# Starting the second expert pass inside the last attention of a macaron block

## What is computed

```python
def ffn(tgt):                      # 8 experts, the best 2 of each row
    logits = tgt @ Wr.T + br
    top_v, top_i = top_k(logits, 2)
    h = relu(tgt @ W1[e].T + b1[e])            # 128 -> 512
    o = h @ W2[e].T + b2[e]                    # 512 -> 128
    return layer_norm(tgt + sum of weight * o) * gamma + beta

def attn(x):                       # per batch
    a1 = softmax(q1 @ k1.T * scale); a2 = softmax(q2 @ k2.T * scale)
    out = (a1 - lam * a2) @ v
    return out / rms(out) * 0.2

x = x + 0.5 * ffn(layernorm(x))
x = x + attn(layernorm(x))
x = x + 0.5 * ffn(layernorm(x))
```

## Time and profile before

| | |
|---|---|
| runs | 649.92 us, median of 3 (648.65 to 650.58) |
| profiled execution | 649.61 us, span 647.9 us |
| TensorE busy | 583.2 us, 90% of the span |
| VectorE, ScalarE, GpSimd busy | 452.0, 446.3, 387.4 us |
| mean granted TensorE clock | 0.959 |
| the last attention | up to about 450 us |
| the second pass | from about 450 us to 614 us |

### The profile page before, as it was taken

One profiled execution on the slowest core, in us unless ns is written; L12 is line 12 of the kernel. 1 busy time (PEld: TensorE's weight loads), 2 busy tenths in 40 slices (PEclk: granted clock), 3 DMA queues, 4 the chain that ended last, 5 costly groups with the idle time before them and its releaser, 6 DMA issues.

```text
span 647.9 us, 16591 instructions
## 1 busy us (share of the span) xinstructions
PE 583.2 (90%) x4362; PEld 536.0 (83%) x4362; DVE 452.0 (70%) x1421; ACT 446.3 (69%) x1224; POOL 387.4 (60%) x481
## 2 busy tenths in 40 slices
PE   5987999999999789898898899887999999899855
PEld 5877999999999678787797788787999999898821
DVE  4784788446684989699779968966647565477635
ACT  4755665766667577677887787675776777787724
POOL 3006565547677785678505486585775777756623
PEclk9588999999999999899999999998999999999958
DMA  8902233223324210000000001021441423630051
GB/s 254 326 12 57 77 77 72 79 69 88 84 68 82 53 30 14 18 24 22 5 2 0 6 30 34 18 69 31 95 103 58 102 79 80 216 95 26 24 194 66
DMA packets 41882, 45.97 MB, mean 71 GB/s; under 512 B 8726, under 2 KB 32706, under 8 KB 41536
## 3 DMA queue, kind: packets, MB, share of 16 engines
q1 hardware_dynamic: 32496, 27.13, 14.6%
q0 software_dynamic: 9088, 17.75, 10.3%
q10 hardware_dynamic: 208, 0.02, 0.0%
HBM read 25.95 MB, written 19.83 MB: 71 GB/s over the span
## 4 chain that ended last, share of the span: by engine, by line
PE 55%; DVE 19%; ACT 8%; issue 7%; POOL 6%; DMA 3%; ACTq 1%; SPq 0%; DVEq 0%; POOLq 0%
PE banks L1074 19%; PE banks L1084 19%; DVE nb L1837 6%; DVE scratch L1844 3%; PE banks L1067 2%; PE banks L1171 2%; PE banks L962 2%; PE banks L964 2%; PE banks L963 2%; POOL rows L499 1%; DVE st_r L1334 1%; POOL zb L512 1%; ACT tgt L649 1%; DVE st_x L1334 1%; DVE mv L1340 1%
## 5 line engine op out<-in xcount | busy, mean ns | idle before, releaser
L1074 PE MATMUL banks<-scratch 128*128 128x128 f32 x1248 | 169.1, 279 | 1.8 <-ACT scratch L706 1.6
L1084 PE MATMUL banks<-blocks,scratch 128*128 x1248 | 166.3, 276 | 2.6 <-ACT scratch L713 1.3
L1587 DVE TENSOR_SCALAR scratch<-banks,blocks 128x128 f32<-128x128 f32 x312 | 95.2, 346 | 91.6 <-PE banks L1074 80.8
L1074 PEld LDWEIGHTS banks<-scratch 128*128 128x128 f32 x1248 | 154.6, 195 | 4.4 <-issue 4.1
L1084 PEld LDWEIGHTS banks<-blocks,scratch 128*128 128x128 f32 x1248 | 151.8, 192 | 4.9 <-issue 4.6
L491 POOL DMA_INDIRECT scratch<-xrows,rowbuf x78 | 75.2, 965 | 82.0 <-DVE rowbuf L1482 41.4
L697 ACT ACTIVATE scratch<-banks 128x128 f32<-128x128 f32 x156 | 43.5, 279 | 88.8 <-PE banks L1067 87.9
L788 ACT ACTIVATE scratch<-banks,nb 128x1024 f32<-128x1024 f32 x64 | 71.3, 1115 | 47.7 <-DVE nb L1837 47.3
L524 POOL DMA_INDIRECT results<-scratch,places x78 | 78.4, 1005 | 34.7 <-issue 21.3
L713 ACT ACTIVATE scratch<-banks,blocks 128x128 f32<-128x128 f32 x312 | 96.8, 366 | 1.2 <-PE banks L1074 1.1
L706 ACT ACTIVATE scratch<-blocks 128x512 f32 x156 | 97.5, 625 | 0.1
(11 more groups left out here) (265 smaller groups left out, 896.5 us busy)
## 6 DMA issues: line engine op xcount, KB each, us to landing
scratch<-rows SPq DMA_DIRECT2D x78, 64.5 KB, 1.9
yrows<-scratch SPq DMA_DIRECT2D x78, 64.0 KB, 1.7
scratch<-in_L_ffn_W_dram SPq DMA_DIRECT2D x1, 2048.0 KB, 20.7
xrows<-tgt SPq DMA_DIRECT2D x4, 512.0 KB, 4.3
x<-in_L_attn_x_dram SPq DMA_DIRECT2D x3, 512.0 KB, 7.9
scratch<-xrows,rowbuf POOLq DMA_INDIRECT x78, 2.6
results<-scratch,places POOLq DMA_INDIRECT x78, 2.4
rows<-padrows SPq DMA_DIRECT2D x18, 64.5 KB
```

What stands on the lines that cost most here:

```text
L1074: ins = pe.matmul(hT_at(T, c), staged(T, c), xT_of(T), start=True, stop=True)
L1084: ins = pe.matmul(y_at(T), hT_of(T, c), blocks[:, W2_AT + c * D:][:, bass.ds(at, D)], start=(c == 0), stop=(c == FC - 1))
L1587: ins = dve.tensor_scalar(hT_of(T, c), hT_at(T, c), blocks[:, B1_AT + c:][:, bass.ds(at, 1)], 0.0, ALU.add, ALU.max)
```

## The change

The first two turns of the second pass and its first product are moved from the head of the pass into the end of the last attention. On TensorE the turn of slot 78 comes ahead of `values` of tile 30, the turn of slot 79 and `first` of slot 78 come ahead of `values` of tile 31, and the pass's loop begins with s = 0 after a wait for `ss_ready` of all 32 tiles. ScalarE's steps -2 and -1 go along, and `copy_rows` of batch 2 comes after them instead of ahead of `take_o` of tile 30. SyncE's one wait on 32 turned tiles becomes three, on 30, 31 and 32 tiles, ahead of the first three loads; for this the three buffers `p1` are used in another order. VectorE's first `add_values` of the last batch moves into the pass's step 0, and the routing of batch 3 moves back by one slot (STATS_AT 1, TURN_AT 9).

```diff
-        STATS_AT, TURN_AT = 0, 8
+        STATS_AT, TURN_AT = 1, 9
...
             group_ready(0)
-            sp.wait_ge(dT_ps, TB * BATCHES)
             for s in range(SLOTS):
+                if s < 3:
+                    sp.wait_ge(dT_ps, TB * BATCHES - 2 + s)
...
# ScalarE, probabilities (and in the same way in turn and difference)
-                    pp, ll = ((p1[t % 3], l1), (p2[t % 2], l2))[m]
+                    pp, ll = ((p1[(t + 2) % 3], l1), (p2[t % 2], l2))[m]
...
# ScalarE, end of the attention
-                if not after:
                     dT_copy(b, TB - 1)
-                    copy_rows(b - 1)
+                    act.wait_ge(table_ready, 3)
+                    step(1, -2)
                     take_o(b, TB - 2)
                     gap(a)
+                    step(1, -1)
+                    copy_rows(b - 1)
                     take_o(b, TB - 1)
...
-            for s in range(-2, SLOTS):
+            for s in range(SLOTS):
                 step(1, s)
...
# TensorE, end of the attention
                     turn(b, TB - 1)
+                    pe.wait_ge(table_ready, 3)
+                    turn_x(SLOTS)
+                    w_at[0] = expert_offset(PE, 0)
                     values(b, TB - 2)
                     prefix(a)
+                    turn_x(SLOTS + 1)
+                    w_at[1] = expert_offset(PE, 1)
+                    first(SLOTS)
                     values(b, TB - 1)
...
-            pe.wait_ge(table_ready, 3)
-            for s in range(-2, SLOTS):
+            pe.wait_ge(ss_ready, TB * BATCHES)
+            for s in range(SLOTS):
...
# VectorE
             def last_route(n):
+                add_values(b, 0)
+                yield
                 add_values(b, 1)
...
-                if not after:
-                    add_values(b, 0)
...
-                if s >= STATS_AT:
+                if s >= STATS_AT - 1:
                     next(routing, None)
```

More of the change, by code:

```diff
@@ L1151, in turn @@
                 for k in range(TB):
-                    ins = pe.transpose(bank(4 + k // 4, (k % 4) * P, (k % 4 + 1) * P), p1[t % 3][:, k * P:(k + 1) * P], ident[:, :])
+                    ins = pe.transpose(bank(4 + k // 4, (k % 4) * P, (k % 4 + 1) * P), p1[(t + 2) % 3][:, k * P:(k + 1) * P], ident[:, :])
                 ins.then_inc(dT_ps, 1)
@@ L1842, in difference @@
                     dve.wait_ge(cc_ready, TB * b + i + 1)
-                    pp = p1[(TB * b + i) % 3]
+                    pp = p1[(TB * b + i + 2) % 3]
                     dve.scalar_tensor_tensor(pp, p2[i % 2], cc[:, c], pp, ALU.mult, ALU.add).then_inc(diff_ready, 1)
```

## The result

The changed kernel takes 658.16 us (median of four runs, 655.88 to 660.13) against 649.28 for the kernel before: 1.0138 times as long, 95% interval 1.0113 to 1.0163, or some 8.9 us more. Its profiled execution took 657.71 us, with a span of 656.0. The forecast was 657.8.

A forecast was written before the change was run, and what follows sets the result against it. TensorE, busy 583 of 647.9 us, was taken to bound the kernel, with the pass started by a load behind GpSimd's last scatter. A shift of +8.2 (6.3 loop, 1.9 slot) on 649.61 gave 657.8 us, range 654.3 to 661.0.

The forecast's parts named there:

- The load isn't released by the split wait but by the last scatter: SyncE at the seam: the split wait is met by 442.4, the scatter's wait ends at 446.83; gain 0.
- 7.3 us of idle time: TensorE ahead of the turn of slot 78: idles from 442.4 to 449.7, waiting for the first load.
- Values of tile 30 at half clock, 3.8 us: TensorE behind the first turn: values of tile 30 take 3.8 us at the low clock, against 2.02 at 2.4 GHz.
- `ss_ready` +8.65, TensorE +5.1 at step 1: End of the seam: last take_o ends at 459.0, not 450.32; step 1's turn comes at 461.1, not 455.98.
- `nm` decides when `make_rows` starts, +8.2, after a wait of 1.4 us: Routing of batch 3: GpSimd's nm ready at 473.65, 1.4 us after ScalarE is ready; make_rows starts at 473.75, +8.2 us.
- The gate 504.7 and the fetch 565.2, both +8.2: GpSimd's first scatter of batch 3 moves from 496.49 to 504.7; batch 0's result comes at 565.2; the loop is +8.2.
- After it TensorE and ScalarE go on as before.: Behind the fetch of batch 0: nothing later gives any of the +8.2 us back; the time from 504 shifts as a block.
- The total: Whole kernel: profiled execution 649.61 us plus 8.2 gives 657.8 us; chance of this case, 656 to 660, 0.62.
- only TensorE's own lateness: Rival: the slot later is swallowed or the clock is high; +5.1 to +6.3, 654.7 to 655.9 us; chance 0.20.
- Its price for a high clock at the seam, 1.9 us: Same rival, values of tile 30 at 2.4 GHz: work from 450.2 to 454 and the end shrink by 1.9 us, +6.3.
- Faster, if the load is there first: Rival at the seam: early rows let turns and product fill the wait, the clock stays high; 646.6 us; chance 0.05.
- Fixed cost of a load: SyncE's first load: lands after 1.80 us by the trace; about 2.0 by the skill, making the sum an estimated +8.4.

The follow-up runs named there:

- e8: The kernel before with only SyncE's wait split into three and the p1 buffers in the other order; 649.13 us, ratio 1.0003.
- e9: The changed kernel without the last three scatters of batch 1, with padding rows written ahead of the attention; 654.62 us, ratio 1.0073.
- e7: The changed kernel with the routing of batch 3 back at its old slots (STATS_AT 0, TURN_AT 8); 658.83 us, ratio 1.0141.
- e4: The changed kernel with 34 transposes of the identity on TensorE ahead of the turn of slot 78; 659.47 us, ratio 1.0154.
- e1: The kernel before with only the routing of batch 3 one slot later and the last batch's add_values inside the pass; 653.52 us, ratio 1.0068.
- e3: The kernel before with GpSimd's last three batch 1 scatters ahead of value_scale and the last batch's first add_values inside the pass; 650.08 us, ratio 1.0006.
- e2: The changed kernel with GpSimd's last three scatters of batch 1 ahead of value_scale of tiles 24 to 27; 655.75 us, ratio 1.0106.
- e5: The changed kernel with values of tile 30 and the prefix ahead of the turn of slot 78, ScalarE likewise; 656.34 us, ratio 1.0113.
- e11: The changed kernel with 62 transposes of the identity on TensorE ahead of the turn of slot 78; 656.98 us, ratio 1.0106.
- e10: The kernel before without the last three scatters of batch 1, with padding rows written ahead of the attention; 654.98 us, ratio 1.0081.

## Why the prediction was right, point by point

- *The load isn't released by the split wait but by the last scatter.* Shown: issued at +6.46 us with the split (e8) and +6.50 without, and with the last three scatters away the first turn is at 0.9 us (e9).
- *7.3 us of idle time.* Measured 7.41. The idle time that it replaces was misread: ahead of the second turn has 0.83 us and not 1.2. Nothing in the sum hangs on it.
- *Values of tile 30 at half clock, 3.8 us.* Measured 3.75, and 2.02 with TensorE kept active. The clock came back 13.6 us after the last turn began, I had 12.6; the product took 1.13 us all the same.
- *`ss_ready` +8.65, TensorE +5.1 at step 1.* Measured +8.5, and the turn of step 1 at 19.8 against 14.6 us, +5.2.
- *`nm` decides when `make_rows` starts, +8.2, after a wait of 1.4 us.* Measured +8.0 with a wait of 0.68. Shown by e7. The wait, for which I had given over 1 us as a sign, was shorter because ScalarE itself was 0.6 us later than in my sum and `nm` 0.2 us sooner.
- *The gate 504.7 and the fetch 565.2, both +8.2.* Measured +8.0 and +8.3. GpSimd waited 3.76 us at the gate, as before, for a later slot table. ScalarE's wait at the fetch, which was to be above 5 us, was 4.53, as ScalarE came there 0.9 us later than in my sum.
- *"After it TensorE and ScalarE go on as before."* Here the sum was off: +9.6 at the end, not +8.3, so the time behind the gate was not shifted as one block. In the changed kernel the stop at the fetch was longer and the clock fell behind it. From ScalarE's start on batch 0's result to the last turn of the pass it is 51.6 us in the four profiles where the clock stayed up there (before, e4, e7, e8; TensorE stood 0.57 to 2.16 us), and 52.9 to 53.2 us in the nine where it fell (2.28 to 3.67 us). So the fall costs 1.3 to 1.6 us. Behind the last turn of the pass it is 38.9 to 39.3 us to the end of the span in all but e4: the changed kernel gets back 0.4 us there (39.0 against 39.3), which leaves +1.3. In e4 the clock fell once more in this last part (a product at 643.94 took 2.04 us behind a stop of 2.84; the same one in e7 took 1.13 us behind 1.94), and it took 40.6 us. The fall at the fetch also explains most of why e1's end is 1.0 us later than its fetch, and why e3's gain came to nothing.
- *The total.* That 657.8 lies 0.4 us from the measured 658.16 is in part luck. Counted from the last turn, the end is 9.6 us later where I had 8.2. But the profiled execution of the changed kernel reached that turn 1.46 us sooner (439.91 against 441.37), by the spread between executions told of above, so that the two profiled executions differ by only 8.1 us; the medians differ by 8.9.
- *Among the rivals,* "only TensorE's own lateness" is out for the changed kernel: its gate and its fetch came late with the sums (+8.5, +8.0, +8.3), and in e2, e5 and e11 all three came sooner together, by 2.0 to 2.4 us. Its price for a high clock at the seam, 1.9 us, was about right: e11 has 2.2. "Faster, if the load is there first" had its condition right and its gain too high: I had 3.0 us ahead of the kernel before (646.6 against 649.61), and e9, counted from the last turn, is 2.2 us ahead at the gate and level at the end of the span.
- *Fixed cost of a load.* The loads land after 1.9 us (median of the changed kernel's 78), near the 1.80 of my row. The Trainium skill, DMA: Bandwidth & Descriptors, Anatomy of one DMA, has about 2.0 us, but for DMAs that GpSimd issues, and SyncE issues these; no run here tests the figure. With the same page's rule to wait on a DMA's semaphore late, under Rules for kernel authors, the changed kernel agrees (the wait ahead of the work, +9 us), and e9 bounds it: where the load has landed, an early wait costs nothing.

## What to carry to other kernels

Before work is pulled ahead of a boundary, find what releases its input, not only which wait stands in front of it: of two waits in a row only the later one is worth splitting. A turn whose load is 7 us away must not stand ahead of work that doesn't need it, and the price is not the idle time but the lateness of the next thing that the other engines go by. A shift that is handed on from gate to gate can grow where the clock falls behind a stop, so a sum of shifts has to take in the stops behind it too.

## What the runs showed of the hardware

- TensorE's granted clock fell to the 1.2 GHz level behind a stop of 2.26 us ahead of the prefix in the kernel before, of 2.28 us at the fetch in e10, of 2.36 us in e3 and of 2.88 us in e7. It stayed at 2.4 GHz through 2.16 us at the fetch in the kernel before and 2.08 in e7, but also through 2.27 us ahead of the prefix in e10 (its lines stand below). So the length of one stop doesn't tell by itself whether the clock falls; what else decides was not tested. A fall at the fetch cost 1.3 to 1.6 us of work on top of the stop.
- Three indirect scatters issued directly behind `ratio` took longer: the first held GpSimd for 2.09 us in e2 and e3 (1.16 in the kernel before, behind the 2.8 us of `value_scale`), and in e3 the last landed after 3.19 us instead of 2.34. The cause was not tested. A reordering on GpSimd that should have gained 2.9 us gained 0.9 to 1.6.
- Transposes of the identity took 0.11 us each at full clock (62 in 6.93 us). With 62 in the wait, which left 0.62 us of idle time behind them, the values ran at full clock; with 34, which left 3.53 us, they ran at half clock as without any.

The stop of e10 ahead of the prefix, and the values of tile 31 behind it at full clock:

```profile
453.21 0.44 PE L1060 MATMUL banks<-cnt,upper 128*128 128x64 f32 x2 [2.27 <-DVE cnt L1517]
...
453.71 2.00 PE L1175 MATMUL banks<-xn,scratch 128*128 128x128 f32 x16
```
